# Spreading the score steps of a slot as two, one, two, and a fourth 512-column difference on ScalarE

## The reference, cut to what matters

```python
x = L0_attn_x                                   # 8 batches x 512 tokens x 128
xn = _layernorm(x, axis=-1)
x = x + attn(xn) + ffn(xn)

# attn: 16 heads of 8 columns
scores = einsum('bhqd,bhkd->bhqk', q, k) / sqrt(8) + causal + logw
#   logw = -log1p(softplus(decay_raw)[h] * log1p(max(i - j, 0)))
att = softmax(scores, axis=-1)
y = einsum('bhqk,bhkd->bhqd', att, v)           # then @ w_proj

# ffn: top 2 of 8 experts, hidden 512, silu
```

## Time and profile before

| | |
|---|---|
| median of three runs | 533.34 us |
| the profiled execution's own time | 531.52 us |
| its span from first to last instruction | 529.1 us |
| PE busy, share of the span | 480.2 us, 91% |
| DVE / ACT / POOL busy | 363.0 / 319.9 / 361.4 us |
| granted TensorE clock, mean | 0.976 |

### The profile page before, as it was taken

One profiled execution on the slowest core, in us unless ns is written; L12 is line 12 of the kernel. 1 busy time (PEld: TensorE's weight loads), 2 busy tenths in 40 slices (PEclk: granted clock), 3 DMA queues, 4 the chain that ended last, 5 costly groups with the idle time before them and its releaser, 6 DMA issues.

```text
span 529.1 us, 13373 instructions
## 1 busy us (share of the span) xinstructions
PE 480.2 (91%) x4316; PEld 349.7 (66%) x4316; DVE 363.0 (69%) x1406; ACT 319.9 (60%) x568; POOL 361.4 (68%) x598
## 2 busy tenths in 40 slices
PE   6777999989999999999999999999999999999920
PEld 5544556555565665565565565565999999999920
DVE  7596987988988878888879879872433333333326
ACT  4578767777877878878877878766233333333300
POOL 3875565556999999987899899891355555555524
PEclk9979999999999999999999999999999999999985
DMA  6566691580460451450461451365466766667349
GB/s 179 171 221 215 172 221 29 157 215 8 136 185 18 140 169 35 140 161 25 138 172 32 137 169 47 94 187 131 125 197 200 209 211 208 207 186 226 113 164 322
DMA packets 71825, 80.37 MB, mean 152 GB/s; under 512 B 8638, under 2 KB 52672, under 8 KB 71760
## 3 DMA queue, kind: packets, MB, share of 16 engines
q1 hardware_dynamic: 67440, 71.06, 46.2%
q0 software_dynamic: 4320, 8.47, 4.5%
HBM read 48.11 MB, written 31.84 MB: 151 GB/s over the span
## 4 chain that ended last, share of the span: by engine, by line
PE 70%; DVE 21%; POOL 3%; DMA 2%; issue 2%; ACT 1%; SPq 0%; DVEq 0%; ACTq 0%; POOLq 0%
PE psT L1291 21%; DVE scores L1121 13%; PE psO L1309 13%; PE ps L1336 12%; PE psT L1363 12%; PE ps L1266 7%; PE psM L1250 2%; POOL xn_all L734 2%; DVE x_all L535 2%; PE ps L1327 1%; DVE xn_all L959 1%; PE psM L1320 1%; POOL rstd L727 1%; DMA probs<-picked_dram 1%; ACT probs L884 1%
## 5 line engine op out<-in xcount | busy, mean ns | idle before, releaser
L1121 DVE CUSTOM_DVE_ANT_0 scores<-ps,wdist 128x256 f32<-128x256 f32 (+3 forms) x512 | 218.4, 486 | 26.9 <-PE ps L1266 24.3
L765 POOL TENSOR_SCALAR scores<-scores,row_max 128x384 f32<-128x384 f32 (+3 forms) x416 | 200.4, 496 | 43.1 <-DVE row_max L1121 41.6
L884 ACT ACTIVATE probs<-psT 128x512 f32<-128x512 f32 x320 | 173.8, 595 | 67.2 <-PE psT L1291 67.2
L1291 PE MATMUL psT<-ident,scores 128*128 128x128 f32 x1280 | 175.8, 280 | 3.7 <-ACT probs L884 3.2
L1291 PEld LDWEIGHTS psT<-ident,scores 128*128 128x128 f32 x1280 | 136.3, 140 | 63.9 <-issue 42.6
L783 POOL DMA_INDIRECT picked_dram<-scores,row_ring x71 | 69.8, 983 | 79.2 <-DVE scores L1173 77.8
L893 ACT ACTIVATE scores<-ps 128x512 f32<-128x512 f32 x71 | 42.4, 597 | 93.8 <-PE ps L1336 93.8
L1309 PE MATMUL psO<-probs,values 128*32 128x512 f32 (+3 forms) x1024 | 82.0, 438 | 0.0
L1336 PE MATMUL ps<-scores,wdist 128*128 128x128 f32 x568 | 75.3, 276 | 0.8 <-DVE scores L1161 0.8
L1363 PE MATMUL psT<-wdist,scores 128*128 x568 | 75.0, 275 | 0.0
L776 POOL DMA_INDIRECT rows_dram<-xn_all x64 | 63.3, 989 | 16.4 <-issue 16.4
(11 more groups left out here) (140 smaller groups left out, 279.3 us busy)
## 6 DMA issues: line engine op xcount, KB each, us to landing
wdist<-w1t SPq DMA_DIRECT2D x71, 256.0 KB, 3.3
k_rows<-k_dram SPq DMA_DIRECT2D x64, 96.0 KB, 2.8
q_rows<-q_dram SPq DMA_DIRECT2D x64, 96.0 KB, 2.6
row_ring<-rows_dram SPq DMA_DIRECT2D x71, 65.0 KB, 3.1
probs<-picked_dram SPq DMA_DIRECT2D x8, 512.0 KB, 6.5
rows_dram<-row_ring SPq DMA_DIRECT2D x7, 585.0 KB, 5.7
k_dram<-k_parts SPq DMA_DIRECT2D x7, 384.0 KB, 2.4
q_dram<-q_parts SPq DMA_DIRECT2D x7, 384.0 KB, 2.6
```

Of the source, the lines that this page charges most:

```text
L765: last = nc.gpsimd.tensor_scalar(part, part, -1.0, row_max[:, r, tile, quad:quad + 1], ALU.mult, ALU.add)
L884: nc.scalar.activation(probs[:, at.ring(2), w, :], psT[:, w % 2], ACT.Exp, scale=-1.0).then_inc(exp_ready, 1)
L1121: last = nc.vector.tensor_tensor_reduce(out=scores[:, r, u, col:col + n], in0=bank[:, col:col + n], in1=wdist[:, at.g * QUADS + quad, SEQ ...
L1291: last = nc.tensor.transpose(psT[:, w % 2, place * P:(place + 1) * P], scores[:, at.ring(2), u, col + key * P:col + (key + 1) * P], ident[:])
```

## The change

Three things change in the list, and one constant. P1(2) moves from behind PV(0), PV(1) and the second TE step to ahead of them, right behind the first TE step; the differences KR and QR and the second TE step follow it. P1(4) moves forward to stand right behind P1(3), and both stand behind the third TE step instead of ahead of it. The differences KL and QL now follow P1(4) too. PV(2) and PV(3) stand behind the fourth TE step instead of ahead of it. Unit 7 goes from POOL to ACT, where it is done together with unit 6 at the slot's end.

PE's order before: P1(0) P1(1) TE KA/QA PV(0) PV(1) TE PJ P1(2) P1(3) TE PV(2) PV(3) TE P1(4) TE.
PE's order after: P1(0) P1(1) TE KA/QA P1(2) TE PV(0) PV(1) PJ TE P1(3) P1(4) TE PV(2) PV(3) TE.

```diff
@@ -107,7 +107,7 @@
-ACT_UNITS = (0, 1, 6)
+ACT_UNITS = (0, 1, 6, 7)
 POOL_UNITS = tuple(u for u in range(UNITS) if u not in ACT_UNITS)
@@ -173,11 +173,12 @@
     step("SA", n, NGROUP, (0, 1))
-    step("PV", n - 2, NGROUP, 0)
-    step("PV", n - 2, NGROUP, 1)
+    p1(2)
     per_batch("KR", -3)
     per_batch("QR", -2)
     step("TE", n - 1, NGROUP, 2, 4)
+    step("PV", n - 2, NGROUP, 0)
+    step("PV", n - 2, NGROUP, 1)
     per_batch("KM", -3)
     per_batch("QM", -2)
@@ -192,20 +193,19 @@
-    p1(2)
+    step("TE", n - 1, NGROUP, 4, 6)
     p1(3)
-    step("TE", n - 1, NGROUP, 4, 6)
+    p1(4)
     per_batch("KL", -3)
     per_batch("QL", -2)
+    step("TE", n - 1, NGROUP, 6, 8)
     step("PV", n - 2, NGROUP, 2)
     step("PV", n - 2, NGROUP, 3)
-    step("TE", n - 1, NGROUP, 6, 8)
     per_batch("KW", -3)
     per_batch("QW", -2)
     per_batch("XT", -4)
-    p1(4)
     step("TE", n - 1, NGROUP, 8, 10)
-    step("SA", n, NGROUP, (6,))
+    step("SA", n, NGROUP, (6, 7))
```

## The result

The changed kernel takes 543.47 us (median of 4 runs, 542.51 to 545.56) against 533.12 us of the kernel before (4 runs, 531.22 to 533.88): a ratio of 1.0212, 95% interval 1.0191 to 1.0234. It is 10.4 us slower. The forecast was 545.8 us, range 537 to 553.

What follows compares the result with a forecast made beforehand. PE was taken as the bound in the slots. Slots 9 to 31 at +10.8 us, slot 32 at +0.7 and slots 2 to 8 at +1.0 made 12.5 us: 545.8 us median, range 537 to 553.

Steps and rivals of the forecast that it cites:

- The 0.27 us of P1(1): PE's hidden wait for E4 ahead of P1(1) goes, a gain of up to 0.27 x 31 = 8.4 us.
- The signs named for it: P1(0) with P1(1) at 0.54; slots about 9.9, 11.5, 10.6, 10.0 us; even-slot waits near 1 us; POOL below 9.
- E0 behind OT: On DVE, OT ahead of E0 delays P1(2) in even slots: waits of 0.96 (n % 4 = 0) and 0.81 us (2).
- QM: Where n % 4 = 2, ACT's copy waits for QR ahead of queued exponentials, delaying the fourth TE by another 0.74 us.
- Unit 7: On ACT, units 6 and 7 delay the next exponential; block 2 waits 0.39 us where n % 4 = 3.
- The clock: PE keeps full clock despite new waits of 0.2 to 1 us, against the skill's warning.
- Slots 2 to 8: Early slots with routing on DVE: losses near 1 us in 2, 6, 8, gains 0.3 to 0.7 elsewhere; +1.0, bounds -5 and +5.
- the cycle: Four successive steady slots, n % 4 = 1, 2, 3, 0: changes of -0.27, +1.27, +0.33, +0.69, together 2.02 us longer.
- GpSimd's relief: Taking unit 7 from POOL frees 0.70 us a slot there, costed at nothing since no PE wait ended with POOL.
- Rivals 2 and 3: Only the 0.27 goes, P1(2) finding E0 done: about 520 us, chance 0.07; gain and loss cancel: 533 us, chance 0.04.
- rival 4: The clock falls to 0.50 in one slot of each cycle: near 590 us, chance 0.02.
- Rival 1: ACT's chains (QM, units 6 and 7) don't reach PE, so waits cost less: 536 to 541 us, chance 0.15.

Runs made afterwards that it cites:

- experiment 5: The changed kernel with only ACT's copies KM and QM moved from ahead of the third TE step to behind it: 538.40 us, ratio 1.0105.
- experiment 1: The kernel before with unit 7 on ACT and nothing moved: 530.89 us, ratio 0.9965.
- experiment 2: The changed kernel with unit 7 back on POOL, so the new order alone: 541.61 us, ratio 1.0153.
- OT alone: The changed kernel with OT moved from the end of odd slots to behind P1(0) of the next: 543.34 us, ratio 1.0182.
- both 12: The changed kernel with OT behind P1(0) of the next slot and KM and QM behind the third TE: 531.64 us, ratio 0.9979.

## Why the prediction was right

- **The 0.27 us of P1(1)** went, as forecast: P1(0) with P1(1) takes 0.53 us in the steady slots, and the slot with n % 4 = 1 fell by 0.37 (10.19 to 9.82) where -0.27 was written; most of the rest is the shorter pitch of P1(2), below. The signs named for it held but for one slot: POOL is at 8.45, 9.09, 7.80 and 8.45 us, and not below 9 where n % 4 = 2.
- **E0 behind OT.** The wait ahead of P1(2) was forecast at 0.96, 0, 0.81 and 0.21 us for n % 4 = 0, 1, 2, 3, and measured 0.91, 0, 0.60 and 0.27.
- **QM.** Forecast 0.74, measured 0.56 in the profile of the changed kernel; experiment 5 prices it at 5 us for the whole, early slots included.
- **Unit 7.** Forecast 0.39 where n % 4 = 3, measured 0.31. In slot 32 the second TE waits 1.07, where the forecast has 2.57 less 1.4, near 1.2.
- **The clock** stayed at 1.00 from 52.71 to 377.10 us, through 45 waits of PE for row maxima and exponentials, the longest of 1.3 us. The Trainium skill's warning in "TensorE: Matmul & The Clock Gate" (section "A second HAM failure mode: psum-queue depth-cycling") about short gaps between groups did not come true in this kernel.
- **Slots 2 to 8** cost 1.75 us, forecast 1.0. The losses in slots 2, 6 and 8 were 0.98, 1.04 and 0.94, as walked; of the gains only that of slot 3 came (0.71), those of slots 4, 5 and 7 were 0.15 to 0.18. Slots 31 and 32 cost 1.19, forecast 1.0.

**The size was off by two terms of the cycle**, both in the same direction. The sum was 12.5 us; the span grew by 11.6 and the median by 10.4. The cycle was walked as 2.02 us longer and is 1.53. First, DVE's steps were taken too long. A pass over 512 columns was taken at its duration of 0.70, while its pitch, where another follows at once, is less: KL starts at 180.69 and OT at 181.29, 0.60 later, and YT takes 0.64 (185.36 to 186.00). OT took 1.48 (181.29 to 182.77) where 1.56 was written, and QM started 0.72 behind the start of QR where 0.80 was. Where n % 4 = 2, all of these stand ahead of QM, and together they make most of the 0.35 us by which this slot was forecast too long (11.47 against 11.12). Second, P1(2) with the switch to the next TE was taken at 0.40 like P1(4), and takes 0.32 (205.34 to 205.66). That shortens the slots with n % 4 = 0 and 1, by most of the 0.10 us that each was below its forecast; in the other two an exponential sets a later TE, and n % 4 = 3 came out 0.06 longer (10.63 against 10.57). Why the two single steps differ was not tried. Slots 9 to 30 so cost 7.7 us where 10.4 were summed. The early slots erred the other way, by 0.75 us, so the total is nearer than its parts, and that is luck.

**A term put at nothing that was not** is GpSimd's relief: in experiment 1 unit 7's move by itself wins 1.9 us (0.5 to 3.2 by the interval), though no wait of PE ended with POOL. In the changed order its share is smaller as far as the waits tell: PE waits 1.0 us less for row maxima than in experiment 2. It too made the sum too large.

Rivals 2 and 3 are excluded by the result, rival 4 by the clock. Rival 1 assumed that the ACT chains don't reach PE; they did: from slot 2 to the first expert tile PE waits 9.2 us for exponentials, against 1.0 before.

## What to carry to other kernels

When engines walk one list, a step that is moved forward on the bound engine must be compared with what stands ahead of its input on each other engine, for every kind of slot: here the eviction was quick, but one slot in two had 1.5 us of output work in front of it. When two chains end at nearly the same time, taking away one can show nothing (OT alone won 0, QM alone 5, both 12); look at the second before giving up the first. And a copy that waits for another engine should stand behind the work of its own engine that is ready, since all behind it waits too.

## What the runs showed of the hardware that was not expected

A few DVE instructions took far longer in the kernel before than in the run with unit 7 alone. The groups of DVE from 50 to 122 us, kernel before, where both have two inputs in SBUF:

```profile
L1035 DVE TENSOR_TENSOR picks<-pick 128x256 bf16<-128x256 f32 x1 | 0.8, 795 | 0.0
L1024 DVE SCALAR_TENSOR_TENSOR masked<-pick,logits 128x256 f32<-128x256 f32 x1 | 0.8, 793 | 0.0
```

and with unit 7 on ACT, nothing moved:

```profile
L1035 DVE TENSOR_TENSOR picks<-pick 128x256 bf16<-128x256 f32 x1 | 0.4, 425 | 0.0
L1024 DVE SCALAR_TENSOR_TENSOR masked<-pick,logits 128x256 f32<-128x256 f32 x1 | 0.4, 424 | 0.0
```

In the kernel before each of the two falls into a GpSimd difference of 512 columns, a unit 7. Here is the first in the timeline, and PE's next wait for a row maximum behind it, ahead of P1(1) of slot 3:

```profile
60.97 0.80 POOL L765 TENSOR_SCALAR scores<-scores,row_max 128x512 f32<-128x512 f32 x1
61.24 0.79 DVE L1024 SCALAR_TENSOR_TENSOR masked<-pick,logits 128x256 f32<-128x256 f32 x1
64.19 0.39 PE L1266 MATMUL ps<-k_rows,q_rows 48*128 48x384 bf16 x4 [1.21 <-DVE row_max L1121]
```

The same two in the run with unit 7 alone, where GpSimd has nothing to do at that moment:

```profile
62.30 0.42 DVE L1024 SCALAR_TENSOR_TENSOR masked<-pick,logits 128x256 f32<-128x256 f32 x1
64.88 0.39 PE L1266 MATMUL ps<-k_rows,q_rows 48*128 48x384 bf16 x4 [0.84 <-DVE row_max L1121]
```

The instruction is 0.37 us shorter and the wait behind it too. So it is with L1035 (0.37, and the wait in slot 4 from 0.69 to 0.32) and with a copy of 128x2 with one input in SBUF (L1050: 0.64 against 0.17 us, inside a GpSimd difference of 512 columns from 93.76 to 94.45; the wait in slot 6 from 1.19 to 0.72). In slot 30 of the kernel before, the last instruction of OT (L1143, two inputs in SBUF) took 1.32 us against 0.48 in the other, beside GpSimd differences from 337.42 to 340.11; it stood ahead of the 0.56 of the earlier trace rows, which is gone there. These four waits make 1.8 of the 2.1 us. Over all 16 instructions L1143 the mean fell from 541 to 477 ns, and PE's waits for row maxima from 5.5 to 3.6 us. The Trainium skill, "SBUF — State Buffer", section "SBUF: two separate sides", says that a VectorE instruction with two SBUF inputs and a GpSimd instruction that reads SBUF exclude each other for their whole length. The three with two SBUF inputs agree with it as far as a trace shows it: L1024 and L1035 end 0.26 and 0.28 us behind the GpSimd instruction beside them. The sentence is not about the copy. All this was read from one execution of each kernel: that the win of experiment 1 comes from fewer such collisions, and not from luck in how the two engines fell together, was not tried by itself.
